# Row maxima of attention scores in two halves of two heads, each with its own count

## The chip, the cores and the metric

The kernel runs on one core of a Trainium2 chip. The metric is the device time of one execution in microseconds (us). TensorE (PE in the profile, its weight loads PEld), VectorE (DVE), ScalarE (ACT), GpSimd (POOL) and SyncE (SP, which issues most of the transfers) each run their own stream of instructions in order. They wait for each other by semaphores, that is counts that one engine raises and another waits for. Matmul results go to PSUM, which has eight banks of 128 partitions x 512 f32 words.

## What is computed

One transformer layer over x of 16 sequences x 512 positions x 128 features. The attention has 16 heads of 8 features:

```python
scores = einsum('bhqd,bhkd->bhqk', Q, K) / sqrt(8)
probs = softmax(scores, axis=-1)
intervened = probs.at[:, :, :, 0].set(0.0)
intervened = intervened / clip(intervened.sum(axis=-1, keepdims=True), 1e-9, None)
combined = probs + 0.5 * (intervened - probs)
attn_out = einsum('bhqk,bhkd->bhqd', combined, V)
x = layernorm(x + attn_out @ Wo.T + bo)
```

After it comes a layer of 8 experts with two chosen per row, and a second layernorm. The softmax subtracts the largest score of each row (query) before the exponential. These row maxima are what the change is about.

## The kernel before, in words

The heads are worked in units of four: 16 sequences x 4 groups make 64 units. A unit's scores are 4 heads x 512 keys x 512 queries. The program walks through periods p from -2 to 63, and each period has eight steps k. In period p three units are in work at once, and each engine writes out the same order by hand:

- the row maxima of unit p + 2 (`maxima`, lines 612 to 623 on TensorE, 1011 to 1018 on VectorE),
- the scores of unit p and their exponentials (`scores`, line 625; `exp_chunk`, line 828),
- the sum of exponentials times values of unit p - 1 (`values`, line 636).

**Row maxima.** A unit has four chunks c of 128 queries. For a chunk TensorE makes four matmuls (line 622), one per head: each has 32 rows of operands and its own PSUM bank of `mx_ps`, and together they give 128 queries x 4 heads x 512 keys. VectorE then reduces all four banks with one instruction (line 1017), the negated maximum of 512 keys for each of four heads. `mx_ps` has these four banks and no second set, so TensorE waits for the reduction of the chunk before (count `s_mx_done`, line 616), and VectorE for the four matmuls (`s_mx_ready`, line 1016). On TensorE the maxima of chunk c stand ahead of the scores in the even step k = 2c (lines 709 and 710).

**Order on TensorE in a chunk** (two steps): maxima, score, score, score, values of four heads, score, and behind it what the table BEHIND puts there (lines 278 and 279): a projection of Q or K for a later sequence (L663), of V (L680), the output projection (L688) or a prefix sum (L693). In step 1 a small transpose (L653) brings the finished maxima of unit p + 1 into rows. Of the 16 chunks of a sequence four have a projection of Q or K, two one of V, two the output projection, one the prefix sum, four the transpose, and three nothing.

**Scores** go through a ring of three PSUM banks (`ring_ps`) that ScalarE empties with one exponential each (line 831); the other jobs use the same ring. A score matmul has 74 rows: the operands and two rows of maxima. Those two rows come by way of the transpose, a copy on ScalarE (line 837), a split on GpSimd (lines 1397 and 1399) and a transfer that SyncE issues (line 472).

**Others that count the maxima.** GpSimd's work is placed beside the reductions: `beside_reduction` (line 1559) waits until the maxima of a given chunk are made. SyncE waits for all chunks of a unit before it loads new operands over the old ones (line 448). VectorE does the rest of its work (transposes, sums, layernorm, routing) between the reductions. In periods -2 and -1 there are no scores yet, and TensorE makes eight more matmuls behind each chunk's maxima (line 714), whose results nobody reads.

After the last unit come the experts and the second layernorm, which the change leaves as they are.

Of the kernel before, what the change touches and what calls it, by code (L numbers as in the profile page):

```python
# [30 lines left out]
QC = L // P  # L31
HG = 4
# [5 lines left out]
MB = 3  # L38
# [20 lines left out]
def layer(nc, xT, x, wqT, wkT, wvT, woT, bq, bk, bv, bo, gateT, w1T, w3T, w2T, out):  # L59
    f32, bf16, i32 = mybir.dt.float32, mybir.dt.bfloat16, mybir.dt.int32  # L60
    ALU, ACT, AXX = mybir.AluOpType, mybir.ActivationFunctionType, mybir.AxisListType.X
# [14 lines left out]
    with ctx:  # L76
        def sb(name, shape, dt=f32):
            return ctx.enter_context(nc.sbuf_tensor(name + "_sb", shape, dt))

        def sem(name):  # L80
            return ctx.enter_context(nc.semaphore(name))
# [33 lines left out]
        rowmax = [sb(f"rowmax{n}", [P, HG * QC]) for n in range(2)]  # L115
# [57 lines left out]
        def psum(name, banks):  # L173
            return ctx.enter_context(nc.psum_tensor(name, [P, banks, L], f32))

        mx_ps = psum("mx_ps", HG)
# [60 lines left out]
        s_mx_ready, s_mx_done = sem("mx_ready"), sem("mx_done")  # L237
# [29 lines left out]
        UNITS, STEPS = NB * NG, 2 * QC  # L267
        PERIODS = range(-2, NB * NG)

        def is_unit(u):  # L270
            return 0 <= u < UNITS

        def is_seq(b):
            return 0 <= b < NB
# [53 lines left out]
        def maxima_in(u):  # L328

            return s_maxima_in[u % MB], MAXIMA_LOADS * (u // MB + 1)  # L330

        def stored(b, which):

            return s_parts_stored[which], STORES[which] * (b + 1)

        def first_stored(which):

            return s_first_stored[which], 16 * (which + 1)
# [15 lines left out]
        def maxima_rows(t, u, r):  # L354

            return t[u % MB][r:P:2, :]

        def maxima_queries(u):

            b, g = divmod(u, NG)  # L360
            first = q_parts_d[b % 2, 0:2, :, HG * g * L:HG * (g + 1) * L]
            return bass.AP(first.tensor, first.offset, [[L, HG], [NH * L, 2 * DK], [1, L]])

        def maxima_keys(u, r):

            b, g = divmod(u, NG)
            first = k_parts_d[b % 2, r:r + 2, :, HG * g * L:HG * (g + 1) * L]
            return bass.AP(first.tensor, first.offset, [[L, HG], [NH * L, 2 * DK], [1, L]])
# [9 lines left out]
        def halves(t):  # L378

            return HALVES if t < FULL else 1  # L380
# [23 lines left out]
        def _(sp):  # L404
# [36 lines left out]
            def load_maxima(u):  # L441

                b, g = divmod(u, NG)
                if g == 0:
                    for which in range(2):
                        sp.wait_ge(*(stored(b, which) if b > 0 else first_stored(which)))
                if u >= MB:
                    sp.wait_ge(s_mx_ready, QC * (u - MB + 1))
                s_loaded = maxima_in(u)[0]
                for r in range(2):  # L450
                    if u > 0:
                        sp.dma_start(maxima_rows(QM, u, r), maxima_queries(u)).then_inc(s_loaded, 16)
                    sp.dma_start(maxima_rows(KM, u, r), maxima_keys(u, r)).then_inc(s_loaded, 16)
# [39 lines left out]
            sp.wait_ge(*split_done(0, 0))  # L493
            sp.dma_start(by_head(q_parts_d[0, 2:3]), qk_parts[0][:, 2:3, :]).then_inc(s_parts_stored[0], 16)
            load_maxima(0)
            load_maxima(1)
            for u in (0, 1):
                load_qk(u)
            load_maxima(2)
            load_xT(2)  # L500
            store_parts(1, 0)
# [31 lines left out]
            sp.wait_ge(s_scattered, SPARE + SENT * ROUTED)  # L533
            sp.wait_ge(s_tab_done, 1)
            sp.wait_ge(s_pv_ready, UNITS - NG)
            sp.wait_ge(s_mx_ready, QC * UNITS)

            def first_row(t):
                return sp.value_load(row0_i[0:1, t:t + 1], min_val=0, max_val=E * REGION + (E - 1) * TK)
# [63 lines left out]
        def _(pe):  # L603

            def ring_bank(*what):

                n = ring_at[what]
                if n >= 3:
                    pe.wait_ge(s_ring_done, n - 2 if n < TAIL else n)
                return bank_of(n)  # L610

            def maxima(u, c):

                n = QC * u + c
                if n >= 1:
                    pe.wait_ge(s_mx_done, n)
                if c == 0:
                    pe.wait_ge(*maxima_in(u))
                q, k = QM[u % MB], KM[u % MB]
                for j in range(HG):  # L620
                    rows = slice(VW * j, VW * (j + 1))
                    last = nc.tensor.matmul(mx_ps[:, j, :], q[rows, P * c:P * (c + 1)], k[rows, :], start=True, stop=True)  # L622
                last.then_inc(s_mx_ready, 1)

            def scores(u, i):

                b, g = divmod(u, NG)
                h, c = HG * g + i // QC, i % QC
                bank = ring_bank("st", u, i)
                if i == 0:  # L630
                    pe.wait_ge(*qk_loaded(u))
                    pe.wait_ge(s_m_loaded[u % 2], 16 * MR * (u // 2 + 1))
                nc.tensor.matmul(bank, KS[b % 2][0:KR + MR, h, P * c:P * (c + 1)],  # L633
                                 QS[b % 2][0:KR + MR, h, :], start=True, stop=True).then_inc(s_ring_ready, 1)

            def values(u, c):

                b, g = divmod(u, NG)
                if c == 0:
                    if u > 0:  # L640
                        pe.wait_ge(s_acc_drained, u)
                    pe.wait_ge(s_v_step, 3 * (b + 1))
                pe.wait_ge(s_ring_done, ring_at["st", u, (HG - 1) * QC + c] + 1)
                for j in range(HG):
                    last = nc.tensor.matmul(acc_ps[VW * j:VW * (j + 1), 0, :], VE[b % 2][:, c, HG * g + j, :],  # L645
                                            PT[u % 2][:, j, c, :], start=(c == 0), stop=(c == QC - 1))
                if c == QC - 1:
                    last.then_inc(s_pv_ready, 1)

            def negmax_to_rows(u):  # L650
                bank = ring_bank("mT", u)
                pe.wait_ge(s_mx_done, QC * (u + 1))
                nc.tensor.transpose(bank[0:HG * QC, 0:P], rowmax[u % 2][:, :], ident[:, :])\  # L653
                  .then_inc(s_ring_ready, 1)

# [49 lines left out]
            for p in PERIODS:  # L705
                b, g = divmod(p, NG)
                for k in range(STEPS):
                    c = k // 2
                    if k % 2 == 0 and is_unit(p + 2):
                        maxima(p + 2, c)  # L710
                        if p + 2 in (0, 1):

                            for n in range(8):
                                nc.tensor.matmul(acc_ps[:, 0, :], QM[p + 2][:, 0:P], KM[p + 2][:, :], start=True, stop=True)  # L714
                    if is_unit(p):
                        scores(p, 2 * k)
                    if k % 2 == 1 and is_unit(p - 1):
                        values(p - 1, c)
                    if is_unit(p):
                        scores(p, 2 * k + 1)  # L720
                    if k == 1 and is_unit(p + 1):
                        negmax_to_rows(p + 1)
                    if (p, k) in ONCE:
                        behind(*ONCE[p, k])
                    if p > -2 and (g, k) in BEHIND:
                        name, off = BEHIND[g, k]
                        if is_seq(b + off):
                            behind(name, b + off)
# [55 lines left out]
                if (t, place) in TAIL_RING:  # L784
                    behind(*TAIL_RING[t, place])

            pe.wait_ge(s_mx_done, QC * UNITS)
            for t in range(TILES + 1):
                if is_tile(t):
                    tile_up(t)  # L790
# [192 lines left out]
        def _(dve):  # L983
            V = nc.vector
# [25 lines left out]

            def maxima(u, c):

                n = QC * u + c
                if c == 0 and u >= 2:
                    dve.wait_ge(s_ring_ready, ring_at["mT", u - 2] + 1)
                dve.wait_ge(s_mx_ready, n + 1)
                V.tensor_reduce(rowmax[u % 2][:, :].rearrange("p (j c) -> p j c", c=QC)[:, :, c], mx_ps[:, :, :], axis=AXX,  # L1017
                                op=ALU.max, negate=True).then_inc(s_mx_done, 1)

            def sums_by_query(u):  # L1020

# [202 lines left out]
            for p in PERIODS:  # L1224
                b, g = divmod(p, NG)
                for k in range(STEPS):
                    if k == 0 and is_unit(p - 2):
                        sums_by_query(p - 2)
                    if k % 2 == 0 and is_unit(p + 2):
                        maxima(p + 2, k // 2)  # L1230
# [84 lines left out]
            for t in range(TILES + 1):  # L1315
# [18 lines left out]
                if is_tile(t):  # L1334
                    dve.wait_ge(s_silu, t + 1)
                    dve.wait_ge(s_lin, t + 1)
                    n = P * halves(t)
# [21 lines left out]
        def _(pool):  # L1359
# [199 lines left out]
            def beside_reduction(p, w):  # L1559

                if is_unit(p + 2):
                    pool.wait_ge(s_mx_ready, QC * (p + 2) + w + 1)

            def chunk(n):
                return n // QC, range(n % QC, n % QC + 1)
# [10 lines left out]
            split_lead(1, 0)  # L1576
            split_rest(1, 0)
            beside_reduction(-1, 1)
            split_negmax(0)
            split_lead(1, 1)  # L1580
# [111 lines left out]
            for b in range(NB):  # L1692
                n = b % 2
# [45 lines left out]
```

## Time and profile before

| | |
|---|---|
| time, median of 3 runs | 1198.48 us |
| the profiled execution's own time | 1199.33 us |
| its span, first to last instruction | 1197.6 us |
| mean granted TensorE clock | 0.986 |
| busy: TensorE, VectorE, ScalarE, GpSimd | 1126.1, 912.3, 827.7, 663.0 us |
| row-maxima reductions | 256, mean 2289 ns, 586.0 us in all |
| score matmuls, exponentials | 1024 each, mean 390 and 598 ns |
| maxima matmuls | 1024, mean 390 ns |

Busy time is the time in which an engine had at least one instruction in work. Instructions on one engine can overlap, so the distance from one start to the next is often shorter than the duration shown. Ends of matmuls are modelled. In the rows a line number such as L622 is a line of the kernel, "x4" is the number of instructions merged into one row, and a bracket such as [0.29 <-DVE rowmax_sb L1017] gives the idle time of the engine ahead of the row and what ended it.

### The profile page before, as it was taken

How to read it: one execution, taken by the hardware profiler on the slowest of the kernel's cores; microseconds unless marked ns; L12 is line 12 of the kernel's file. 1: busy time of each engine (PE TensorE's matmuls, PEld its weight loads, DVE VectorE, ACT ScalarE, POOL GpSimd, SP SyncE). 2: the span in 40 equal slices, each digit the busy share in tenths (PEclk: the TensorE clock that was granted, in tenths of full speed). 3: DMA queues.
4: the chain of work that ended last, by engine and by line, in shares of the span. 5: the costliest groups of instructions: out<-in, count | busy, mean ns of one | idle time of the engine just before them, and what ended most of it. 6: DMA issues, size and time to landing. Idle time of an engine off the chain costs nothing.

```text
span 1197.6 us, 23394 instructions
## 1 busy us (share of the span) xinstructions
PE 1126.1 (94%) x7185; PEld 569.2 (48%) x7189; DVE 912.3 (76%) x1322; ACT 827.7 (69%) x1689; POOL 663.0 (55%) x1003
## 2 busy tenths in 40 slices
PE   7799999999999999999999999899999999999985
PEld 5222222222222222222222222279999999999952
DVE  6688999999999999999999999854545543443334
ACT  1378889889888889888888888844544434435635
POOL 2523456676676676676676654666545433333345
PEclk9799999999999999999999999999999999999998
DMA  4443334343343343443443344353334333321156
GB/s 145 129 124 129 112 107 133 120 130 124 126 132 122 120 137 107 140 131 107 139 128 114 126 149 144 100 113 83 84 78 104 85 77 78 78 59 40 43 189 236
DMA packets 162954, 138.40 MB, mean 116 GB/s; under 512 B 77443, under 2 KB 139527, under 8 KB 162832
## 3 DMA queue, kind: packets, MB, share of 16 engines
q1 hardware_dynamic: 153576, 118.57, 34.6%
q0 software_dynamic: 8688, 18.14, 4.5%
q8 instruction: 60, 0.98, 0.4%
q14 instruction: 62, 0.51, 0.1%
q10 hardware_dynamic: 568, 0.20, 0.1%
HBM read 94.59 MB, written 42.19 MB: 114 GB/s over the span
## 4 chain that ended last, share of the span: by engine, by line
PE 46%; DVE 38%; issue 9%; DMA 3%; SPq 1%; POOL 1%; ACT 1%; ACTq 0%; DVEq 0%; POOLq 0%
DVE rowmax_sb L1017 30%; PE ring_ps L776 11%; PE mx_ps L757 10%; PE mx_ps L747 9%; PE ring_ps L633 5%; PE acc_ps L645 4%; DVE TN_sb L1026 3%; PE mx_ps L622 3%; PE ring_ps L680 1%; PE mx_ps L808 1%; DVE stats_sb L1049 1%; DVE meanvar_sb L1056 1%; PE ring_ps L688 1%; PE acc_ps L714 1%; DMA out<-probs_sb 1%
## 5 line engine op out<-in xcount | busy, mean ns | idle before, releaser
L831 ACT ACTIVATE probs_sb<-ring_ps 128x512 f32<-128x512 f32 x1024 | 558.0, 598 | 105.6 <-PE ring_ps L633 90.2
L1017 DVE TENSOR_REDUCE rowmax_sb<-mx_ps 128x4 f32<-128x2048 f32 x256 | 586.0, 2289 | 36.2 <-PE mx_ps L622 30.6
L633 PE MATMUL ring_ps<-region_sb 74*128 74x512 bf16 x1024 | 314.9, 390 | 7.3 <-DMA region_sb<-negmax_parts_sb 5.2
L645 PE MATMUL acc_ps<-probs_sb,values_sb 128*32 128x512 f32 x2048 | 273.2, 606 | 0.5 <-DVE TN_sb L1026 0.5
L1688 POOL DMA_INDIRECT y_d<-probs_sb,values_sb x135 | 133.0, 985 | 196.6 <-DVE probs_sb L1330 172.4
L633 PEld LDWEIGHTS ring_ps<-region_sb 74*128 74x128 bf16 x1024 | 79.6, 97 | 323.7 <-ACT probs_sb L831 275.1
L906 ACT ACTIVATE xT_sb<-region_sb 128x512 f32 x78 | 49.2, 630 | 186.0 <-PE mx_ps L757 184.6
L1544 POOL DMA_INDIRECT rows_d<-sent_sb,pos_sb x128 | 130.1, 1016 | 41.2 <-issue 19.3
L1338 DVE TENSOR_TENSOR probs_sb<-mx_ps,probs_sb 128x1024 f32<-128x1024 f32 (+1 forms) x78 | 84.3, 1081 | 78.2 <-PE mx_ps L757 78.2
L622 PE MATMUL mx_ps<-k_maxima_sb,q_maxima_sb 32*128 32x512 bf16 x1024 | 102.4, 390 | 44.1 <-DVE rowmax_sb L1017 38.9
L776 PE MATMUL ring_ps<-region_sb,probs_sb 128*128 x1080 | 136.0, 278 | 3.0 <-DMA region_sb<-w2T 1.5
L1330 DVE SCALAR_TENSOR_TENSOR probs_sb<-ring_ps,values_sb 128x128 f32<-128x128 f32 x135 | 42.1, 347 | 121.8 <-issue 77.3
L776 PEld LDWEIGHTS ring_ps<-region_sb,probs_sb 128*128 128x128 f32 x1080 | 127.0, 192 | 14.4 <-issue 7.2
L747 PE MATMUL mx_ps<-k_parts_sb,xT_sb 128*128 128x256 f32 (+1 forms) x624 | 130.2, 352 | 0.0
L747 PEld LDWEIGHTS mx_ps<-k_parts_sb,xT_sb 128*128 128x128 f32 x624 | 106.9, 191 | 12.3 <-DVE k_parts_sb L1312 0.8
L645 PEld LDWEIGHTS acc_ps<-probs_sb,values_sb 128*32 128x32 f32 x2048 | 40.6, 108 | 99.0 <-issue 98.1
L622 PEld LDWEIGHTS mx_ps<-k_maxima_sb,q_maxima_sb 32*128 32x128 bf16 x1024 | 25.9, 91 | 116.2 <-DVE rowmax_sb L1017 101.4
L958 ACT ACTIVATE probs_sb<-mx_ps 128x1024 f32<-128x1024 f32 (+1 forms) x78 | 70.4, 903 | 3.6 <-PE mx_ps L747 3.5
L757 PE MATMUL mx_ps<-k_parts_sb,full_q_sb 128*128 128x256 f32 (+1 forms) x312 | 65.6, 353 | 0.0
L757 PE MATMUL mx_ps<-k_parts_sb,full_k_sb 128*128 128x256 f32 (+1 forms) x312 | 64.6, 350 | 0.0
L1397 POOL CAST negmax_parts_sb<-negmax_sb 16x128 bf16<-16x128 f32 x64 | 17.9, 280 | 70.4 <-PE mx_ps L622 57.7
L757 PEld LDWEIGHTS mx_ps<-k_parts_sb,full_q_sb 128*128 128x128 f32 x312 | 51.7, 191 | 5.3 <-issue 0.8
(190 smaller groups left out, 1170.6 us busy)
## 6 DMA issues: line engine op xcount, KB each, us to landing
region_sb<-q_parts_d SPq DMA_DIRECT2D x64, 288.0 KB
region_sb<-k_parts_d SPq DMA_DIRECT2D x64, 288.0 KB
k_parts_d<-k_parts_sb SPq DMA_DIRECT2D x46, 256.0 KB, 2.8
k_maxima_sb<-k_parts_d SPq DMA_DIRECT2D x128, 64.0 KB
probs_sb<-y_d SPq DMA_DIRECT2D x32, 256.0 KB, 5.4
q_maxima_sb<-q_parts_d SPq DMA_DIRECT2D x126, 64.0 KB
values_sb<-rows_d SPq DMA_DIRECT2D x57, 132.0 KB, 2.2
q_parts_d<-q_parts_sb SPq DMA_DIRECT2D x15, 384.0 KB, 3.6
```

The costliest lines, as they stand in the source:

```text
L622: last = nc.tensor.matmul(mx_ps[:, j, :], q[rows, P * c:P * (c + 1)], k[rows, :], start=True, stop=True)
L633: nc.tensor.matmul(bank, KS[b % 2][0:KR + MR, h, P * c:P * (c + 1)], QS[b % 2][0:KR + MR, h, :], start=True, stop=True).then_inc(s_ring_re ...
L645: last = nc.tensor.matmul(acc_ps[VW * j:VW * (j + 1), 0, :], VE[b % 2][:, c, HG * g + j, :], PT[u % 2][:, j, c, :], start=(c == 0), stop=( ...
L747: last = nc.tensor.matmul(up_ps[:, c, 0:n], W1T[t % 2][:, P * c:P * (c + 1)], XGT[t % 2][:, 0:n], start=True, stop=True)
L757: last = nc.tensor.matmul(lin_ps[:, c, 0:n], W3T[t % 2][:, P * c:P * (c + 1)], XGT[t % 2][:, 0:n], start=True, stop=True)
L776: last = nc.tensor.matmul(y_ps[:, at:at + D], HH[t % 2][:, c, P * w:P * (w + 1)], W2[:, bass.ds(expert + c * D, D)], start=(c == 0), stop= ...
L831: nc.scalar.activation(PT[u % 2][:, i // QC, i % QC, :], ring_bank("st", u, i), ACT.Exp, scale=SCALE).then_inc(s_ring_done, 1)
L958: nc.scalar.activation(SG[t % 2][:, :, 0:n], up_ps[:, :, 0:n], ACT.Silu).then_inc(s_silu, 1)
L1017: V.tensor_reduce(rowmax[u % 2][:, :].rearrange("p (j c) -> p j c", c=QC)[:, :, c], mx_ps[:, :, :], axis=AXX, op=ALU.max, negate=True).the ...
L1338: V.tensor_tensor(HH[t % 2][:, :, 0:n], lin_ps[:, :, 0:n], SG[t % 2][:, :, 0:n], ALU.mult)\
L1544: G.indirect_dma_start(rows_d, bass.IndirectOffsetOnAxis(ap=pos[b % 2][:, s, c:c + 1], axis=0), XE[b % 2][:, c, s, :], None).then_inc(s_sc ...
L1688: G.indirect_dma_start(y_d, bass.IndirectOffsetOnAxis(ap=XG[t % RING][:, w, D:D + 1].bitcast(i32), axis=0), YO[t % YRING][:, w, :], None, ...
```

## The change

Each chunk's maxima are made in two halves s = 0 and 1: heads 0 and 1 (banks 0 and 1), then heads 2 and 3 (banks 2 and 3). TensorE makes the first half in the even step and the second in the odd step, so that between the two stand two score matmuls, and behind the second half come a score, the values and the last score. A half waits for the reduction of the same half of the chunk before (one reduction may still be open). VectorE reduces each half with an instruction of its own, one behind the other. Both counts run to twice their old values, and all who wait for them are changed accordingly; GpSimd waits for the second half of its chunk. The matmuls of line 714 become four behind each half.

```diff
-            def maxima(u, c):
-
-                n = QC * u + c
-                if n >= 1:
-                    pe.wait_ge(s_mx_done, n)
-                if c == 0:
+            def maxima(u, c, s):
+
+                n = 2 * (QC * u + c) + s
+                if n >= 2:
+                    pe.wait_ge(s_mx_done, n - 1)
+                if c == 0 and s == 0:
                     pe.wait_ge(*maxima_in(u))
                 q, k = QM[u % MB], KM[u % MB]
-                for j in range(HG):
+                for j in (2 * s, 2 * s + 1):
...
-                    if k % 2 == 0 and is_unit(p + 2):
-                        maxima(p + 2, c)
+                    if is_unit(p + 2):
+                        maxima(p + 2, c, k % 2)
                         if p + 2 in (0, 1):
 
-                            for n in range(8):
+                            for n in range(4):
...
             def maxima(u, c):
 
-                n = QC * u + c
+                n = 2 * (QC * u + c)
                 if c == 0 and u >= 2:
                     dve.wait_ge(s_ring_ready, ring_at["mT", u - 2] + 1)
-                dve.wait_ge(s_mx_ready, n + 1)
-                V.tensor_reduce(rowmax[u % 2][:, :].rearrange("p (j c) -> p j c", c=QC)[:, :, c], mx_ps[:, :, :], axis=AXX,
-                                op=ALU.max, negate=True).then_inc(s_mx_done, 1)
+                for s in range(2):
+                    heads = slice(2 * s, 2 * s + 2)
+                    dve.wait_ge(s_mx_ready, n + s + 1)
+                    V.tensor_reduce(rowmax[u % 2][:, :].rearrange("p (j c) -> p j c", c=QC)[:, heads, c],
+                                    mx_ps[:, heads, :], axis=AXX, op=ALU.max, negate=True).then_inc(s_mx_done, 1)
...
                 if is_unit(p + 2):
-                    pool.wait_ge(s_mx_ready, QC * (p + 2) + w + 1)
+                    pool.wait_ge(s_mx_ready, 2 * (QC * (p + 2) + w + 1))
```

## Rows read from the trace of the kernel before

**Rows 1.** The page: busy time by engine, and the chain that ended last by line.

```profile
PE 1126.1 (94%) x7185; PEld 569.2 (48%) x7189; DVE 912.3 (76%) x1322; ACT 827.7 (69%) x1689; POOL 663.0 (55%) x1003
...
DVE rowmax_sb L1017 30%; PE ring_ps L776 11%; PE mx_ps L757 10%; PE mx_ps L747 9%; PE ring_ps L633 5%; PE acc_ps L645 4%; DVE TN_sb L1026 3%; PE mx_ps L622 3%; PE ring_ps L680 1%; PE mx_ps L808 1%; DVE stats_sb L1049 1%; DVE meanvar_sb L1056 1%; PE ring_ps L688 1%; PE acc_ps L714 1%; DMA out<-probs_sb 1%
```

**Rows 2.** Stretches: length, busy of PE, PEld, DVE, ACT, POOL, clock, DMA, GB/s.

```profile
48.00:66.00 18.00, 16.87 (x61) 3.66 (x61) 10.67 (x5) 12.13 (x25) 4.91 (x8) 0.52 0.32 100
...
400.00:500.00 100.00, 95.33 (x637) 28.76 (x634) 97.32 (x113) 87.06 (x186) 69.31 (x109) 1.00 0.39 124
```

**Rows 3.** Line 622, from 66 to 756 us: durations, first and last start.

```profile
L622 PE MATMUL mx_ps<-k_maxima_sb,q_maxima_sb x968: 383/385/386, 67.3 to 752.2; 32*128 32x512 bf16 x194
```

**Rows 4.** VectorE in order of time, from 422.8 to 431 us.

```profile
422.90 2.29 DVE L1017 TENSOR_REDUCE rowmax_sb<-mx_ps 128x4 f32<-128x2048 f32 x1
425.11 0.70 DVE L1026 STREAM_TRANSPOSE TN_sb<-acc_ps 128x512 f32<-128x512 f32 x1
425.77 2.29 DVE L1017 TENSOR_REDUCE rowmax_sb<-mx_ps 128x4 f32<-128x2048 f32 x1
...
428.57 2.29 DVE L1017 TENSOR_REDUCE rowmax_sb<-mx_ps 128x4 f32<-128x2048 f32 x1 [0.22 <-PE mx_ps L622]
```

**Rows 5.** Waits from 200 to 700 us: total, times, longest.

```profile
PE mx_ps L622 <- DVE rowmax_sb L1017: 25.7, 82, 0.4
...
DVE rowmax_sb L1017 <- PE mx_ps L622: 2.5, 11, 0.2
```

**Rows 6.** TensorE in order of time: a chunk with a projection behind it.

```profile
408.30 0.40 PE L622 MATMUL mx_ps<-k_maxima_sb,q_maxima_sb 32*128 32x512 bf16 x4
408.62 0.82 PE L633 MATMUL ring_ps<-region_sb 74*128 74x512 bf16 x3
409.37 1.07 PE L645 MATMUL acc_ps<-probs_sb,values_sb 128*32 128x512 f32 x8
410.37 0.39 PE L633 MATMUL ring_ps<-region_sb 74*128 74x512 bf16 x1
410.60 0.60 PE L663 MATMUL ring_ps<-xT_sb,wq_sb 128*128 128x256 f32 x2
411.13 0.40 PE L622 MATMUL mx_ps<-k_maxima_sb,q_maxima_sb 32*128 32x512 bf16 x4
```

**Rows 7.** TensorE: a chunk's end with nothing, and one with the transpose behind.

```profile
424.53 0.39 PE L633 MATMUL ring_ps<-region_sb 74*128 74x512 bf16 x1
425.25 0.40 PE L622 MATMUL mx_ps<-k_maxima_sb,q_maxima_sb 32*128 32x512 bf16 x4 [0.33 <-DVE rowmax_sb L1017]
...
427.56 0.28 PE L653 MATMUL ring_ps<-ident_sb,rowmax_sb 128*16 128x128 f32 x1
428.12 0.39 PE L622 MATMUL mx_ps<-k_maxima_sb,q_maxima_sb 32*128 32x512 bf16 x4 [0.29 <-DVE rowmax_sb L1017]
```

**Rows 8.** TensorE in order of time, from 47 to 60 us.

```profile
47.70 1.88 PE L633 MATMUL ring_ps<-region_sb 74*128 74x512 bf16 x4 [5.23 <-DMA region_sb<-negmax_parts_sb]
...
59.28 0.61 PE L622 MATMUL mx_ps<-k_maxima_sb,q_maxima_sb 32*128 32x512 bf16 x4 [0.56 <-DVE rowmax_sb L1017]
59.83 1.46 PE L633 MATMUL ring_ps<-region_sb 74*128 74x512 bf16 x3
```

**Rows 9.** Groups of VectorE, 200 to 700 us: busy us, mean ns, idle before.

```profile
L1017 DVE TENSOR_REDUCE rowmax_sb<-mx_ps 128x4 f32<-128x2048 f32 x177 | 405.0, 2288 | 7.0 <-PE mx_ps L622 2.5 <-issue 0.2
...
L1080 DVE TENSOR_REDUCE top_sb<-logits_sb 128x4 f32<-128x32 f32 x22 | 3.9, 176 | 0.0
```

**Rows 10.** All engines in order of time, from 405 to 414.5 us.

```profile
405.96 0.28 POOL L1397 CAST negmax_parts_sb<-negmax_sb 16x128 bf16<-16x128 f32 x1 [1.02 <-PE mx_ps L622]
...
406.77 1.21 SPq L472 DMA_DIRECT2D region_sb<-negmax_parts_sb  x2
...
409.05 1.58 ACT L831 ACTIVATE probs_sb<-ring_ps 128x512 f32<-128x512 f32 x3
```

**Rows 11.** Transfers issued from 200 to 700 us: number, size, median us to landing.

```profile
region_sb<-negmax_parts_sb SPq DMA_DIRECT2D x88, 4.0 KB, 1.8
```

More of the change, by code:

```diff
@@ L447, in load_maxima @@
                 if u >= MB:
-                    sp.wait_ge(s_mx_ready, QC * (u - MB + 1))
+                    sp.wait_ge(s_mx_ready, 2 * QC * (u - MB + 1))
                 s_loaded = maxima_in(u)[0]
@@ L535, in _ @@
             sp.wait_ge(s_pv_ready, UNITS - NG)
-            sp.wait_ge(s_mx_ready, QC * UNITS)
+            sp.wait_ge(s_mx_ready, 2 * QC * UNITS)
             def first_row(t):
@@ L651, in negmax_to_rows @@
                 bank = ring_bank("mT", u)
-                pe.wait_ge(s_mx_done, QC * (u + 1))
+                pe.wait_ge(s_mx_done, 2 * QC * (u + 1))
                 nc.tensor.transpose(bank[0:HG * QC, 0:P], rowmax[u % 2][:, :], ident[:, :])\
@@ L785, in beside @@
                     behind(*TAIL_RING[t, place])
-            pe.wait_ge(s_mx_done, QC * UNITS)
+            pe.wait_ge(s_mx_done, 2 * QC * UNITS)
             for t in range(TILES + 1):
```

## The prediction, made before the changed kernel was run

> **What bounds the kernel now.** I read the page first. TensorE is busy for 94% of the span and VectorE for 76%, and of the chain that ended last the one line of the row maxima has 30% [rows 1]. Averages over stages mislead here, so the table of stretches came next: from 400 to 500 us VectorE is busy for 97% of the time and TensorE for 95% [rows 2]. Two engines are nearly full at once, and the question is how much room each has in the stage that the change touches, and how much the change asks of each.
>
> The stage is a train of equal chunks, one per reduction: four maxima matmuls (called M here), four score matmuls (S), one group of eight records for the values (V), and mostly one small job behind the last S. From 67.3 to 752.2 us there are 968 M records, so 242 chunks [rows 3]; (752.2 - 67.3) / 241 = 2.842 us each.
>
> *VectorE in a chunk.* A reduction lasts 2.29 us, but the next instruction starts 2.21 us after it (422.90 to 425.11), and the other work fills the time in which TensorE refills: the transpose of 425.11 ends at 425.81, where the next reduction has already begun. Only where little other work stands does VectorE wait, 0.22 us before 428.57 [rows 4]. In 500 us these waits come to 2.5 us, 11 times [rows 5]. So the refill gap, which looks like 0.5 us in each chunk, is filled already: VectorE needs 0.973 x 2.842 = 2.77 us of the 2.842.
>
> *TensorE in a chunk.* Starts from 408.30 on [rows 6]: M 408.30, first S 408.62 (0.32), V 409.37 (0.75 for three S), fourth S 410.37 (1.00), the projection behind it 410.60 (0.23), next M 411.13 (0.53). Sum 2.83, with no idle time noted: a chunk with a long job behind it is TensorE's own length. Elsewhere TensorE waits. With nothing behind (422.46 to 425.25) the fourth S starts at 424.53 and M at 425.25, 0.72 later, where 0.31 would do (the third S at 409.05, which is 408.62 + 0.82 - 0.39, is 0.32 before V): 0.41 free. With the small transpose behind (427.56, next M 428.12) 0.36 is free: half of the 0.22 that one 256-column pass of the projection takes (0.60 - 0.38) and 0.09 for the change of shape stand against 0.56 [rows 7].
>
> By the table BEHIND the 241 chunks are 110 with a long job (52 q/k, 58 v/wo), 13 with the small prefix job (about 0.1 free), 60 with a transpose, 58 with nothing. Free in all: 60 x 0.36 + 58 x 0.41 + 13 x 0.1 = 47 us, or **0.20 us a chunk**. The table of waits gives the same size: 25.7 us noted as idle before M in 500 us, 0.146 a chunk, and some 0.04 more because ends are modelled late [rows 5].
>
> **The change, part by part.**
>
> *The second group of maxima on TensorE.* M becomes M0 (heads 0 and 1) and M1 (heads 2 and 3), and M1 stands between the second and third S. The four matmuls of M run side by side on four groups of 32 rows: four records in 0.40 us, one of them alone 0.385 [rows 3, 6]. Two therefore take as long as four, and M0 saves next to nothing. M1 is a second pass. Today S follows S after 0.215 (three in 0.82). With M1 between them it is S to M1, 0.31 by the nearest row (third S to V, a change from whole array to narrow tiles), and M1 to S, 0.32 (M to first S): 0.31 + 0.32 - 0.215 = **0.42 us a chunk on TensorE**.
>
> Why a change of shape costs 0.1 is seen in the rows: S to S is 0.215, S to V 0.32, M to S 0.32, and M, S and V have different row and column extents. The Trainium skill has a rule for it: TensorEngine Tiling (Array Packing), Key Properties, says that changing the tiling mode drains TensorE. It gives no price. The rows do, 0.1 a change of shape, and a chunk goes from four such changes to six. By that rule the sum is the 0.42; without it 0.215, the first rival.
>
> Bounds of this term: below, 0.215 (M1 costs its 512 columns and no more) or even nothing, if a pair streams beside S on rows that S leaves free; above, 0.42 x 0.55 / 0.32 = 0.7, the ratio at which M stands to S when the clock is low [rows 6, 8]. I take 0.42, since each transition has a row of its kind.
>
> *The reduction in two.* The slope is (2288 - 176) ns over 2016 elements, 1.048 ns each, by the large and the small reduction [rows 9]; 1024 elements make 176 + 992 x 1.048 = 1.22 us. If the second starts 0.08 before the end of the first, as after 2.21 of 2.29, the pair holds VectorE for 1.14 + 1.22 = 2.36, 0.07 more than now; if it starts only after it, 2.44 and some 0.04 for the count, 0.19 more. VectorE then needs 2.84 to 2.96 a chunk. I take 2.84: the next instruction overlaps in every row.
>
> *What the waits do.* M0 of the next chunk waits for the first half of this one, which ends 1.2 us after it begins, so on TensorE M0 and M1 are free long before their turn. The refill gap goes; late next is TensorE's own sequence. Queued behind a waiting M1 would be S, V and through them ScalarE; it should not wait. ScalarE has room: three exponentials take 1.58 us and one 0.6 (598 ns in the table above), so they start 0.49 apart [rows 10] and four need 2.0 of a chunk; with a longer chunk the score banks come free earlier against TensorE's order, not later.
>
> *The chunk after.* TensorE asks 2.842 - 0.195 + 0.42 = 3.07 on average: about 3.25 with a long job, 2.93 with the transpose, 2.80 with nothing. VectorE's 2.84 is below it, and half a chunk of slack (it may lag by over 1 us before M0 waits) evens out neighbours. The stage is TensorE's: 685 - 47 + 241 x 0.42 = 739, so **+54 us**.
>
> *Edges.* From 48 to 66 us the granted clock is 0.52, the lower level (1.2 GHz) nearly throughout, after 5.23 us in which TensorE did nothing; five chunks lie there. At 0.7 each, less the 0.56 that each of two such chunks has free before its M, they add 2 us [rows 2, 8]. Before 47.7 the start waits for a transfer, not for TensorE; the warm-up matmuls keep their number: 0, at most 8 x 0.35 = 3 if the cover goes. GpSimd's waits now count M1, which is 0.85 later in its chunk: the split of the maxima began at 405.96, its transfer was issued at 406.77 and lands 1.8 us later, over 5 us before the scores that need it, in the chunk behind that of 411.13, at about 414.3 [rows 6, 10, 11]: 0; were that cover gone, each us late would cost 64. SyncE waits for whole units and is not moved. After 752.2 no maxima are made: 0.
>
> **Sum.** The profiled execution took 1199.33 us for a span of 1197.6; 1199.3 + 54 + 2 = **1255 us**. It lies 0.85 above the median of 1198.48, so nothing is to be corrected.
>
> **Rivals.**
> 1. *M1 costs only its columns.* TensorE then asks 2.65 (2.842 - 0.195) and 0.215, together 2.86, VectorE 2.84 to 2.90; stage 241 x 2.89 = 697, +12: 1211 us. For it: weights of one group can be in place early, as between S and S. Against it: no S next to an M in the rows is under 0.31. A rule of the Trainium skill would lead here: TensorE: Matmul & The Clock Gate, Part 3, The mechanism, has weights pulled ahead when row groups do not conflict. Here S has 74 rows and M1 uses rows 64 to 127, so at most one of its two groups is clear.
> 2. *VectorE becomes the bound too.* If the halves do not overlap and each chunk takes the longer of the two engines, VectorE's 2.96 stands against TensorE's 2.80 in 58 chunks and 2.93 in 60: 58 x 0.16 + 60 x 0.03 = 11 more, 1266 us. For it: the second half waits for a count of its own. Against it: instructions with waits that are already met overlap now.
> 3. *Not slower: the refill gap is what counts.* If a pair streams beside S and TensorE's extra stays under the 0.20 it has free (that is the point where it decides), VectorE sets the pace. Without refill waits it needs 2.77 to 2.84: 0 to 0.07 less in 241 chunks, 1182 to 1199, near 1195. For it: the long chain share of the reductions. Against it: VectorE waits 2.5 us in 500, so hardly anything can be won, and two passes take twice the columns of one.
>
> **How the numbers follow.** Forecast 0.75, first rival 0.12, second 0.09, third 0.04. The forecast's own range is 1228 (S to M1 without its change of shape: 0.31 a chunk, 27 us less) to 1270 (0.06 a chunk, 15 us, for small waits at score banks or halves). For 8 in 10 I take 1226 to 1275: the second rival is inside, the first and third are left out (0.16). A measurement of this kernel tells about 2%, 24 us, from no change. Forecast and second rival are slower by more: 0.84. The first and half of the third are within: 0.14. Faster gets the other 0.02.
>
> **What would show it.** Right: reductions of about 1.22 us, twice as many; some 0.63 between the second and third S of a chunk; M without idle time before it; VectorE waiting for M 0.2 to 0.4 us in chunks with a long job, its busy share near 92%; chunks of 3.07. Wrong: M1 under 0.25 behind S, or TensorE still waiting for reductions, or 2.9 a chunk.

## The result, and the profile after

| | before | changed |
|---|---|---|
| the profiled execution | 1199.33 us | 1260.32 us |
| its span | 1197.6 us | 1258.6 us |
| median | 1198.48 us | 1261.85 us |
| busy TensorE, VectorE | 94%, 76% | 98%, 75% |

The changed kernel takes 1.0544 times as long as the one before (95% interval 1.0505 to 1.0584); the ratio compares means, 1262.2 us of four runs with 1197.1 us of two, since two further runs of the kernel before took 2699 us in a slow state and are left out. The profiled execution is 61.0 us longer. 1255 was predicted, with a range of 1226 to 1275; 56 of the 61 us were foreseen.

The page of the changed kernel, first the busy line, then the chain that ended last by engine, then the group of the reductions, and below them the wait of VectorE for the maxima from 200 to 700 us (total, times, longest, as in [rows 5]):

```profile
PE 1231.9 (98%) x7185; PEld 594.1 (47%) x7189; DVE 939.1 (75%) x1578; ACT 824.0 (65%) x1689; POOL 663.3 (53%) x1003
...
PE 91%; DMA 2%; DVE 1%; POOL 1%; SPq 1%; issue 1%; ACT 1%; ACTq 0%; POOLq 0%; DVEq 0%
...
L1019 DVE TENSOR_REDUCE rowmax_sb<-mx_ps 128x2 f32<-128x1024 f32 x512 | 603.6, 1219 | 73.2 <-PE mx_ps L622 72.2
...
DVE rowmax_sb L1019 <- PE mx_ps L622: 33.1, 100, 0.6
```

The chain has turned over. Before, one line of VectorE had 30% of it [rows 1]; now VectorE has 1% and TensorE 91%. The reductions are twice as many at 1219 ns, and from 200 to 700 us VectorE waits 33.1 us for the matmuls of line 622, where it had waited 2.5 us [rows 5]. The table of stretches (columns as in [rows 2]) says the same for a steady part:

```profile
400.00:500.00 100.00, 100.00 (x578) 29.34 (x576) 92.38 (x135) 79.01 (x171) 63.09 (x100) 1.00 0.37 115
```

TensorE is recorded as never idle, and 578 matmul records fit into 100 us where there were 637 [rows 2]. TensorE in order of time, a chunk with the output projection behind it, the chunk with the transpose, and the one after that:

```profile
433.17 0.39 PE L622 MATMUL mx_ps<-k_maxima_sb,q_maxima_sb 32*128 32x512 bf16 x2
433.49 0.60 PE L633 MATMUL ring_ps<-region_sb 74*128 74x512 bf16 x2
434.03 0.39 PE L622 MATMUL mx_ps<-k_maxima_sb,q_maxima_sb 32*128 32x512 bf16 x2
434.35 0.39 PE L633 MATMUL ring_ps<-region_sb 74*128 74x512 bf16 x1
434.67 1.06 PE L645 MATMUL acc_ps<-probs_sb,values_sb 128*32 128x512 f32 x8
435.67 0.39 PE L633 MATMUL ring_ps<-region_sb 74*128 74x512 bf16 x1
435.89 0.63 PE L688 MATMUL ring_ps<-wo_half_gate_sb,attnT_sb 128*128 128x136 f32 x4
436.45 0.39 PE L622 MATMUL mx_ps<-k_maxima_sb,q_maxima_sb 32*128 32x512 bf16 x2
...
439.18 0.28 PE L653 MATMUL ring_ps<-ident_sb,rowmax_sb 128*16 128x128 f32 x1
439.38 0.39 PE L622 MATMUL mx_ps<-k_maxima_sb,q_maxima_sb 32*128 32x512 bf16 x2
439.70 0.71 PE L633 MATMUL ring_ps<-region_sb 74*128 74x512 bf16 x2
440.35 0.39 PE L622 MATMUL mx_ps<-k_maxima_sb,q_maxima_sb 32*128 32x512 bf16 x2
```

Call the two halves M0 and M1, a score S and the values V, as in the prediction. M0 at 433.17 takes as long to the first S (0.32) as the whole M did [rows 6]. The second S starts 0.22 after the first, at 433.71; M1 follows at 434.03, 0.32 later, and the third S 0.32 after that. The second and third S stand 0.64 apart, against 0.215 before. The chunk is 3.28 us long, against 2.83 in [rows 6]: M1 and the two transitions around it add 0.42, and the job at the end is another one (0.56 from its start to the next M0, against 0.53). The last rows show something else: in the chunk behind a transpose the two S are recorded over 0.71 us and not 0.60, and M1 starts 0.65 behind the first S and not 0.54. That 0.11 is taken up below.

The ledger of the 61.0 us, by the first matmul of M in chosen chunks: ahead of chunk 14 (67.3 before, 69.6 after) +2.3; the 241 chunks from there to the last (684.9 before; after, from 69.65 to 815.97) +61.4; from the start of the last chunk's maxima to the end -2.7.

### The profile page after: what moved, and what is told of

Same layout as the page of the kernel before. It is cut to its first block, busy times and chain, and to the rows that moved or that the text cites. A ratio compares the mean times of both kernels' runs of the same rounds, so it can differ in the third digit from the quotient of the medians.

```text
span 1258.6 us, 23650 instructions
## 1 busy us (share of the span) xinstructions
PE 1231.9 (98%) x7185; PEld 594.1 (47%) x7189; DVE 939.1 (75%) x1578; ACT 824.0 (65%) x1689; POOL 663.3 (53%) x1003
## 3 DMA queue, kind: packets, MB, share of 16 engines
q1 hardware_dynamic: 153576, 118.57, 33.1%
## 4 chain that ended last, share of the span: by engine, by line
PE 91%; DMA 2%; DVE 1%; POOL 1%; SPq 1%; issue 1%; ACT 1%; ACTq 0%; POOLq 0%; DVEq 0%
PE ring_ps L633 24%; PE acc_ps L645 19%; PE mx_ps L622 13%; PE ring_ps L776 10%; PE mx_ps L757 9%; PE mx_ps L747 9%; PE ring_ps L663 2%; PE mx_ps L808 1%; PE ring_ps L680 1%; PE ring_ps L688 1%; PE ring_ps L653 1%; SPq L548 0%; PE acc_ps L714 0%; DMA region_sb<-negmax_parts_sb 0%; DMA probs_sb<-y_d 0%
## 5 line engine op out<-in xcount | busy, mean ns | idle before, releaser
L1019 DVE TENSOR_REDUCE rowmax_sb<-mx_ps 128x2 f32<-128x1024 f32 x512 | 603.6, 1219 | 73.2 <-PE mx_ps L622 72.2
L633 PE MATMUL ring_ps<-region_sb 74*128 74x512 bf16 x1024 | 363.8, 392 | 4.3 <-DMA region_sb<-negmax_parts_sb 2.2
L633 PEld LDWEIGHTS ring_ps<-region_sb 74*128 74x128 bf16 x1024 | 83.6, 96 | 350.4 <-ACT probs_sb L831 257.0
L622 PE MATMUL mx_ps<-k_maxima_sb,q_maxima_sb 32*128 32x512 bf16 x1024 | 201.0, 389 | 4.5 <-DMA k_maxima_sb<-k_parts_d 4.5
L622 PEld LDWEIGHTS mx_ps<-k_maxima_sb,q_maxima_sb 32*128 32x128 bf16 x1024 | 48.1, 91 | 166.0 <-issue 123.7
```

## The experiments

The theory is that M1, set apart from M0, is a second pass on TensorE with two more changes of shape, and that TensorE then sets the stage alone. Its rival is that the two reductions, with twice the counts and waits, make the loss.

**Less work for VectorE, in the changed kernel and in the one before.** Both leave out half of each row maximum: it is taken over the first 256 keys.

```diff
-                                    mx_ps[:, heads, :], axis=AXX, op=ALU.max, negate=True).then_inc(s_mx_done, 1)
+                                    mx_ps[:, heads, 0:L // 2], axis=AXX, op=ALU.max, negate=True).then_inc(s_mx_done, 1)
```

> The changed kernel, with each of its 512 reductions over the first 256 of the 512 keys only: half of each reduction is left out, all else stays. Theory 1 (the second group of maxima is a second pass on TensorE with two changes of shape, 0.41 us a chunk, and TensorE alone sets the stage): VectorE gets some 0.54 us x 512 = 270 us less to do and the time stays, 1258 to 1264 us, chunks of 3.1. Rival (two reductions in place of one, or the waits for them, make the loss): below 1240 us.

Measured: 1263.86 us median, 1.0551 (1.0525 to 1.0576) of the kernel before, against 1.0544 for the whole reductions. The stretch from 400 to 500 us of this run:

```profile
400.00:500.00 100.00, 100.00 (x578) 29.36 (x577) 70.13 (x135) 79.11 (x171) 63.16 (x101) 1.00 0.37 115
```

VectorE falls from 92 to 70% busy, TensorE's 578 records stay, and so does the time. In the changed kernel VectorE sets nothing, so neither the second reduction nor what it costs can be the loss. The counts and the waits are all kept in this run; they are tried below, with the halves side by side.

> The kernel before, with each of its 256 reductions over 256 of the 512 keys: half of each is left out. It measures the room that TensorE had. Theory 1 (0.20 us a chunk free on TensorE, VectorE the other bound): 47 us less, perhaps 7 of them given back to score banks behind the transposes: 1150 to 1160 us, and projections still 2.83 to 2.86 a chunk. Rival (TensorE was the only bound before): 1190 us or more. Rival (VectorE alone was, with far more room on TensorE): below 1130 us.

Measured: 1160.17 us, 0.969 (0.9671 to 0.9709), 37 us less than the kernel before on the same chip (1197.04). TensorE in order of time, a chunk behind a transpose and one with nothing behind:

```profile
397.62 0.40 PE L622 MATMUL mx_ps<-k_maxima_sb,q_maxima_sb 32*128 32x512 bf16 x4
397.95 0.99 PE L633 MATMUL ring_ps<-region_sb 74*128 74x512 bf16 x3
398.87 1.07 PE L645 MATMUL acc_ps<-probs_sb,values_sb 128*32 128x512 f32 x8
399.87 0.39 PE L633 MATMUL ring_ps<-region_sb 74*128 74x512 bf16 x1
400.10 0.60 PE L663 MATMUL ring_ps<-xT_sb,wk_sb 128*128 128x256 f32 x2
400.63 0.40 PE L622 MATMUL mx_ps<-k_maxima_sb,q_maxima_sb 32*128 32x512 bf16 x4
...
403.03 0.40 PE L622 MATMUL mx_ps<-k_maxima_sb,q_maxima_sb 32*128 32x512 bf16 x4
...
405.43 0.40 PE L622 MATMUL mx_ps<-k_maxima_sb,q_maxima_sb 32*128 32x512 bf16 x4
```

With VectorE out of the way the empty chunk is 2.40 us long, where it was 2.79 (422.46 to 425.25, the chunk of [rows 7]). TensorE's room in the kernel before was real, and of the size that the prediction gave: 47 us, less what the banks take back (three S over 0.99 us in the first chunk, against 0.82 in [rows 6]). Chunks of one kind are about 0.10 longer behind a transpose than elsewhere in this run, 6.3 us in all 60. The time lies 0.2 us above the range that was expected.

**One change of shape less.** M1 moves from ahead of the third score to directly ahead of the values.

```diff
-                    if is_unit(p + 2):
-                        maxima(p + 2, c, k % 2)
+                    if k % 2 == 0 and is_unit(p + 2):
+                        maxima(p + 2, c, 0)
...
                     if is_unit(p):
                         scores(p, 2 * k)
+                    if k % 2 == 1 and is_unit(p + 2):
+                        maxima(p + 2, c, 1)
...
                     if k % 2 == 1 and is_unit(p - 1):
                         values(p - 1, c)
```

> The changed kernel, with the second half of the maxima moved on TensorE from ahead of the third score to directly ahead of the values, so that a chunk has five changes of shape and not six. Theory 1 (every change of shape costs about 0.1 us, narrow to narrow too): second half to values 0.32 us, 0.10 a chunk less, about 1238 us. Rival 1a (only a change from or to the whole array costs): second half to values 0.22, 0.2 a chunk less, about 1214 us. Rival 1b (the second half costs only its pass, wherever it stands): 1262 us.

Measured: 1239.62 us, 1.0356 (1.0335 to 1.0377), 22 us less than the changed kernel. The 241 chunks are 25 us shorter (746.3 to 721.1), 0.105 each, and start 3.6 us later. An empty chunk of this run:

```profile
448.95 0.39 PE L622 MATMUL mx_ps<-k_maxima_sb,q_maxima_sb 32*128 32x512 bf16 x2
449.27 0.82 PE L633 MATMUL ring_ps<-region_sb 74*128 74x512 bf16 x3
450.03 0.39 PE L622 MATMUL mx_ps<-k_maxima_sb,q_maxima_sb 32*128 32x512 bf16 x2
450.35 1.06 PE L645 MATMUL acc_ps<-probs_sb,values_sb 128*32 128x512 f32 x8
451.35 0.39 PE L633 MATMUL ring_ps<-region_sb 74*128 74x512 bf16 x1
451.67 0.39 PE L622 MATMUL mx_ps<-k_maxima_sb,q_maxima_sb 32*128 32x512 bf16 x2
```

and one of the changed kernel:

```profile
458.36 0.39 PE L622 MATMUL mx_ps<-k_maxima_sb,q_maxima_sb 32*128 32x512 bf16 x2
...
461.18 0.39 PE L622 MATMUL mx_ps<-k_maxima_sb,q_maxima_sb 32*128 32x512 bf16 x2
```

M1 to V is 0.32 (450.03 to 450.35), as much as M to S: a change between two narrow shapes costs as much as one from the whole array, and rival 1a falls with 1b. Three empty chunks without any wait now give the prices apart: 2.40 with M whole, 2.72 with M1 beside V, 2.82 with M1 between scores. One change of shape is 0.10 us; the pass with one change is 0.32, so the pass alone is 0.22. What the 0.10 consists of stays open: each of these changes also has a load of weights ahead of it (0.09 to 0.11 us in the records), and no run tells that load from anything else that TensorE may do there.

**The 0.11 behind a transpose.** In the changed kernel, all engines in order of time behind the transpose at 439.18:

```profile
439.38 0.60 ACT L831 ACTIVATE probs_sb<-ring_ps 128x512 f32<-128x512 f32 x1 [0.54 <-PE ring_ps L633]
...
439.70 0.10 PEld L633 LDWEIGHTS ring_ps<-region_sb 74*128 74x128 bf16 x1 [0.23 <-issue]
...
440.03 0.10 PEld L633 LDWEIGHTS ring_ps<-region_sb 74*128 74x128 bf16 x1 [0.23 <-ACT probs_sb L831]
```

The exponential ends at 439.98, and the weight load of the second S starts 0.05 later, put down to it. With three banks the ring goes: last S of the chunk, transpose, first S, second S. The second S gets the bank of that last S, whose exponential has only just ended. All 60 chunks behind a transpose in the steady part have this wait: the second S starts 0.325 behind the first on average, and 0.226 in the other chunks. To test it, the transpose goes ahead of the last score, on TensorE, ScalarE and in the ring's order:

```diff
-                    if is_unit(p):
-                        scores(p, 2 * k + 1)
                     if k == 1 and is_unit(p + 1):
                         negmax_to_rows(p + 1)
+                    if is_unit(p):
+                        scores(p, 2 * k + 1)
```

> The changed kernel, with the transpose of the finished maxima moved ahead of the last score of its step, on TensorE, ScalarE and in the order of the ring. In the changed kernel the second score of the chunk behind a transpose starts 0.325 us after the first and not 0.226. Theory 2 (that score waits for its bank, whose exponential is that of the score just ahead of the transpose): the 0.11 us go in 60 chunks, 6 to 7 us less, about 1255 us. Rival (the bank is not the reason): no change, 1260 us or more.

Measured: 1256.73 us, 1.049 (1.0469 to 1.0512), 5 us less than the changed kernel. The same place in this run:

```profile
439.80 0.39 PE L624 MATMUL mx_ps<-k_maxima_sb,q_maxima_sb 32*128 32x512 bf16 x2
440.12 0.60 PE L635 MATMUL ring_ps<-region_sb 74*128 74x512 bf16 x2
440.66 0.39 PE L624 MATMUL mx_ps<-k_maxima_sb,q_maxima_sb 32*128 32x512 bf16 x2
```

The pair of scores is back to 0.60 and M1 to 0.54 behind the first of them. The intervals of the two kernels overlap a little, so the time alone would not settle it; the rows do. The wait is gone behind all 60 transposes, and with it 6.6 us. The 241 chunks gain only 4.6 (746.3 to 741.7), as the first of them (71.03 to 76.79) still ran at a granted clock of 0.50 and took 2.5 us more than others of its kind.

**The halves side by side.** M1 directly behind M0; the counts, waits and reductions of the change stay.

```diff
-                    if is_unit(p + 2):
-                        maxima(p + 2, c, k % 2)
+                    if k % 2 == 0 and is_unit(p + 2):
+                        maxima(p + 2, c, 0)
+                        maxima(p + 2, c, 1)
...
```

> The changed kernel, with the second half of the maxima directly behind the first on TensorE (both in the even step); counts, waits and the two reductions stay as they are. Theory 1 (the loss is the second pass and its two changes of shape, because the halves stand apart): side by side they have no score between them and no extra change of shape; if TensorE comes late they even run together. TensorE needs 2.65 to 2.87 us a chunk, VectorE about 2.84 with a pair at 2.24 to 2.27 us: 1195 to 1212 us. Rival (two reductions, twice the counts and the waits on them make the loss): 1240 us or more.

Measured: 1197.89 us against 1197.59 for the kernel before, 1.0002 (0.9993 to 1.0011). The whole loss is gone, with 512 reductions and all the counts in place. Its stretch from 400 to 500 us, VectorE in order of time, and two groups of maxima on TensorE:

```profile
400.00:500.00 100.00, 99.52 (x635) 30.21 (x633) 97.97 (x148) 86.69 (x185) 69.73 (x107) 1.00 0.42 127
```

```profile
423.00 2.36 DVE L1020 TENSOR_REDUCE rowmax_sb<-mx_ps 128x2 f32<-128x1024 f32 x2
425.27 0.18 DVE L1083 TENSOR_REDUCE top_sb<-logits_sb 128x4 f32<-128x32 f32 x1
425.49 0.19 DVE L1087 SCALAR_TENSOR_TENSOR dist_sb<-logits_sb,top_sb 128x32 f32<-128x32 f32 x1
425.71 0.19 DVE L1092 SCALAR_TENSOR_TENSOR absl_sb<-dist_sb,rev_sb 128x32 f32<-128x32 f32 x1
425.82 1.22 DVE L1020 TENSOR_REDUCE rowmax_sb<-mx_ps 128x2 f32<-128x1024 f32 x1
```

```profile
422.57 0.40 PE L622 MATMUL mx_ps<-k_maxima_sb,q_maxima_sb 32*128 32x512 bf16 x4
...
424.97 0.83 PE L622 MATMUL mx_ps<-k_maxima_sb,q_maxima_sb 32*128 32x512 bf16 x4
```

VectorE is at 98%, the next pair begins before the other work has ended, and there is next to nothing left to win by refilling earlier. TensorE's 99.5% is not all work: where it is late, both halves run together (422.57), and where it is early, M1 waits for its reduction and stands 0.4 to 0.5 us behind M0 (424.97), which it does in 113 of the 241 chunks. A pair holds VectorE for 2.27 us (423.00 to 425.27) where one reduction held it for 2.21 [rows 4].

**The second reduction by itself.** TensorE as before, VectorE in halves, and each wait for the whole chunk.

```diff
-                    pe.wait_ge(s_mx_done, n)
+                    pe.wait_ge(s_mx_done, 2 * n)
...
-                V.tensor_reduce(rowmax[u % 2][:, :].rearrange("p (j c) -> p j c", c=QC)[:, :, c], mx_ps[:, :, :], axis=AXX,
-                                op=ALU.max, negate=True).then_inc(s_mx_done, 1)
+                for s in range(2):
+                    heads = slice(2 * s, 2 * s + 2)
+                    V.tensor_reduce(rowmax[u % 2][:, :].rearrange("p (j c) -> p j c", c=QC)[:, heads, c],
+                                    mx_ps[:, heads, :], axis=AXX, op=ALU.max, negate=True).then_inc(s_mx_done, 1)
```

> The kernel before on TensorE (four maxima matmuls with one count, ahead of them a wait for the whole chunk before), with VectorE's reduction in two halves. The price of the second reduction by itself. In the changed kernel the second of a pair starts 1.14 us after the first and what follows 1.13 later, 0.06 more than the 2.21 of one whole reduction, where the prediction had 0.07. Theory 1: some 0.03 to 0.07 us in 241 chunks, less where TensorE is late anyway: 1203 to 1214 us. Rival (the second reduction is a main part of the loss): 1230 us or more.

Measured: 1208.98 us, 1.0094 (1.008 to 1.0107): 11 us, or 0.047 a chunk. That is the price of cutting the reduction where VectorE sets the pace, and side by side the early refill gives it back: there the 241 chunks are only 1.1 us longer than in the kernel before, here 10.7.

**The last candidate.** Halves side by side and the transpose ahead of the last score.

> The kernel with both halves side by side on TensorE, and the transpose of the finished maxima ahead of the last score of its step, which took the wait of the second score away in the changed kernel. The likeliest of these to beat the kernel before. Theory 1 (VectorE sets the stage here, so time taken from TensorE buys nothing): within 4 us of the one without the transpose moved. Rival (score banks still cost here): 5 to 7 us less than that one.

Measured: 1198.88 us, 1.0011 (1.0002 to 1.002), 1 us from the one without the transpose moved. The run is no test of what the wait costs there, for it had nothing to remove: with the halves side by side the second S stands 0.226 behind the first after all 60 transposes already. Of the versions that compute the whole maxima none beats the kernel before.

## Why the prediction was right, and where it was not

The mechanism was right: a second pass with two changes of shape, and TensorE then alone in setting the stage. The step that failed is a term that the sum put at 0, the wait for score banks; it measured 6.6 us.

- *VectorE's refill gap is filled already.* Right in the main. With the gap closed and the reduction cut (side by side) the time is the same to 0.1%. Cutting alone costs 11 us, so closing the gap does return some 10 us, 0.04 a chunk, and the cut takes them.
- *TensorE has 0.20 us a chunk free, 47 us.* Right in size: 37 us showed, and 7 of the other 10 were expected to go to the banks. In the small prefix job the 0.1 that was called free is mostly not there: in the changed kernel its chunk is 3.185 us long, 0.39 more than the 2.80 before, so that 0.03 was free; that makes 1 us in 13 chunks.
- *M1 adds 0.42: a pass of 0.215 and two changes of shape of 0.1.* Right: 2.82 against 2.40 in empty chunks, and the pass and the change were told apart at 0.22 and 0.10. The rule that was weighed, in the Trainium skill's TensorEngine Tiling (Array Packing), Key Properties, that a change of tiling mode drains TensorE, agrees with all of these transitions. Whether the 0.10 is that drain no run here shows.
- *The reduction in two: 1.22 us each, 0.07 more for a pair.* Right for one (1219 ns). The pair holds VectorE for 0.06 more; by itself it cost 0.047 a chunk, as some chunks wait for TensorE anyway.
- *"With a longer chunk the score banks come free earlier against TensorE's order, not later."* This step failed, and with it the 0 that the sum had for the banks; only the range had room for them. It went by the average time that ScalarE needs in a chunk, and by chunks in which TensorE waited ahead of M for VectorE (0.36 us behind the transpose, [rows 7]); that wait hid the one at the bank. When M no longer waits, only 0.98 us (0.23 + 0.21 + 0.32 + 0.22) would lie between the last S of the chunk with a transpose (438.95) and the second S after it, and the score, its exponential and the counts between need 1.08 (to 440.03). The runs bear this out: the wait is behind all 60 transposes where M does not wait for VectorE (the changed kernel, and the kernel before with short reductions), and behind none in the kernel before or with the halves side by side. 60 chunks x 0.11 = 6.6 us: that and the prefix job are the difference between +54 and the measured +61.4 in the 241 chunks.
- *Edges +2.* The +2.3 at the start is luck. Five slow chunks with an M1 each were to make +2. The first four of them took 1.0 us more, but had begun 0.9 us earlier, so that the fifth, chunk 13, began at 63.96 against 63.84. Chunk 13 itself is 2.2 us longer, mostly by the clock, which rose later: the granted clock was 1.00 from 66 us on before, and in the changed kernel 0.50 until 68 and 0.66 from 68 to 70. The values of that chunk, first in the kernel before, then in the changed one:

```profile
65.54 1.07 PE L645 MATMUL acc_ps<-probs_sb,values_sb 128*32 128x512 f32 x8
...
66.54 1.94 PE L645 MATMUL acc_ps<-probs_sb,values_sb 128*32 128x512 f32 x8
```

  With the halves side by side, where no score stands between them, the clock is as late (0.57 from 68 to 70), chunk 13 is 1.7 us longer than before, and chunk 14 begins at 69.85, as late as in the changed kernel. The -2.7 at the end is not put down to the change: from the start of the last chunk's maxima to the end it took 445.4 us before and 442.6 after, but 445.5 in the changed kernel with short reductions, which has the same order on TensorE.
- *The rivals.* M1 at its columns alone (1211) falls by the measured 0.10 for each change. VectorE as a second bound (1266) falls with the short reductions, which did not make the changed kernel faster. "Not slower" needed TensorE's extra under 0.20; it is 0.42, and even without a score between the halves (side by side) the gain is zero.

## What to carry to other kernels

Count a chunk on each engine from start to start, and compare what a change adds with the room that each engine has there: a gap in which an engine does its other work is hardly a gap. Small matmuls that run side by side on separate rows are one pass; set apart, they are two, and each change of tile shape between them cost 0.10 us on top, at the full clock. When a wait goes, look for the one that it hid: here a ring of three banks was one bank short as soon as TensorE stopped waiting elsewhere.

## What was not expected of the hardware

With short reductions in the changed kernel, some of VectorE's small instructions with two inputs in SBUF grew from some 0.2 to between 0.8 and 1.1 us. All engines in order of time:

```profile
451.53 1.16 POOL L1414 TENSOR_TENSOR full_q_sb<-full_q_sb,q_parts_sb 128x512 f32<-128x512 f32 x1
451.62 1.12 DVE L1086 SCALAR_TENSOR_TENSOR dist_sb<-logits_sb,top_sb 128x32 f32<-128x32 f32 x1
452.77 0.19 DVE L1091 SCALAR_TENSOR_TENSOR absl_sb<-dist_sb,rev_sb 128x32 f32<-128x32 f32 x1
```

VectorE's instruction begins 0.09 us behind GpSimd's and ends 0.05 us behind its end (452.74 to 452.69). From 200 to 700 us of that run all 50 instructions of lines 1086, 1104, 1111 and 1130 end so, within 0.1 us behind a two-input instruction of GpSimd. The Trainium skill's SBUF — State Buffer, SBUF: two separate sides, says that the two engines share a pair of ports which one of them holds for a whole instruction; these rows agree. The kernel places GpSimd's work beside the reductions, which read PSUM; a change that shifts the reductions against the counts that GpSimd waits for undoes that. It cost nothing here, as VectorE had time to spare.
